# The state-space output map multiplied into the cell's input weights on chip, and later states made between the cell's steps

## The reference, cut to what matters

```python
    def _L2_cond_ref(x, conv_w, conv_b, Wp, bp, Ws, bs, A_log, dt_log, Wo, bo):
        conv = conv_b + sum((x_pad[:, k:k + L, :] * conv_w[k, 0] for k in range(K)))
        proj = conv @ Wp + bp
        B_t = jax.nn.softplus(proj[..., :N])
        C_t = jnp.tanh(proj[..., N:])
        u = x @ Ws + bs
        def step(state, inputs):
            state = decay * state + dt * b_t * u_t
            return (state, c_t * state)
        y = jnp.swapaxes(ys, 0, 1)
        return y @ Wo + bo

    def _L2_ffn_ref(x, wf, uf, bf, wi, ui, bi, wc, uc, bc, wo, uo, bo, in_c):
        def step(c, xt):
            ft = jax.nn.sigmoid(xt @ wf.T + c @ uf.T + bf)
            it = jax.nn.sigmoid(xt @ wi.T + c @ ui.T + bi)
            gt = jnp.tanh(xt @ wc.T + c @ uc.T + bc)
            c = ft * c + it * gt
            return (c, None)
        c_final, _ = lax.scan(step, c0, x)
        h = jnp.tanh(jnp.einsum('tbi,oi->tbo', x, wo) + c_final @ uo.T + bo)
```

## Time and profile before

| what | before |
|---|---|
| median of 3 runs | 3221.84 us (3221.58 to 3226.26) |
| time of the profiled execution | 3220.31 us |
| its span | 3218.6 us |
| TensorE busy | 88% of the span |
| DVE, ACT, POOL busy | 43%, 27%, 13% |
| mean granted TensorE clock | 0.764 of full speed |
| share of the chain that ended last: PE | 76% |

### The profile page before, as it was taken

One profiled execution on the slowest core, in us unless ns is written; L12 is line 12 of the kernel. 1 busy time (PEld: TensorE's weight loads), 2 busy tenths in 40 slices (PEclk: granted clock), 3 DMA queues, 4 the chain that ended last, 5 costly groups with the idle time before them and its releaser, 6 DMA issues.

```text
span 3218.6 us, 73352 instructions
## 1 busy us (share of the span) xinstructions
PE 2819.7 (88%) x28032; PEld 2120.7 (66%) x28032; DVE 1385.8 (43%) x6805; ACT 867.4 (27%) x2721; POOL 404.5 (13%) x477
## 2 busy tenths in 40 slices
PE   7888888888888888439999998999979997999788
PEld 5777777777777777128888887556843342586467
DVE  5555555555555555201111111664435565412532
ACT  1222222222222222222322222113533222322332
POOL 1000000000000000341111111333420000001333
PEclk6555555555555555659999998999989999899999
DMA  9990000000000000146666666223453210000023
GB/s 312 379 354 4 2 2 2 2 2 2 2 2 2 2 2 2 47 134 203 195 184 206 190 189 190 90 75 96 138 168 126 104 54 0 0 0 0 28 82 102
DMA packets 218204, 295.94 MB, mean 92 GB/s; under 512 B 57688, under 2 KB 160704, under 8 KB 216704
## 3 DMA queue, kind: packets, MB, share of 16 engines
q1 hardware_dynamic: 200640, 243.80, 23.1%
q0 software_dynamic: 17344, 48.78, 4.2%
HBM read 167.59 MB, written 124.94 MB: 91 GB/s over the span
## 4 chain that ended last, share of the span: by engine, by line
PE 76%; DVE 8%; ACT 6%; issue 4%; POOL 3%; DMA 1%; SPq 0%; DVEq 0%; POOLq 0%; ACTq 0%
PE bank L1548 20%; PE bank L1656 8%; PE bank L1668 8%; PE bank L1532 8%; PE bank L1932 5%; PE bank L1740 4%; ACT gate_r L663 3%; DVE rhpart L992 3%; PE bank L1838 3%; PE bank L1882 3%; PE bank L1791 2%; PE bank L1802 2%; POOL tile_rows L607 2%; PE bank L2033 2%; PE bank L2045 2%
## 5 line engine op out<-in xcount | busy, mean ns | idle before, releaser
L1548 PE MATMUL bank<-h_high,WB 128*128 128x8 f16 x9216 | 422.3, 169 | 87.2 <-DVE h_high L1008 67.3
L1548 PEld LDWEIGHTS bank<-h_high,WB 128*128 128x128 f16 x9216 | 335.6, 105 | 204.3 <-DVE h_high L1008 165.7
L1548 PE MATMUL bank<-rhpart,WB 128*128 128x8 f16 x6144 | 288.2, 171 | 84.6 <-DVE rhpart L992 84.6
L1548 PEld LDWEIGHTS bank<-rhpart,WB 128*128 128x128 f16 x6144 | 242.8, 106 | 130.0 <-DVE rhpart L992 127.9
L1656 PE MATMUL bank<-WA,WB 128*128 128x256 f32 x1248 | 310.3, 382 | 7.3 <-DMA WA<-in_L_ffn_b 7.3
L1668 PE MATMUL bank<-WB,hid 128*128 128x256 f32 x1248 | 313.9, 379 | 0.0
L1532 PE MATMUL bank<-XT,WB 128*128 128x128 f32 x792 | 304.5, 482 | 0.0
L1548 PE MATMUL bank<-h_low,WB 128*128 128x8 f16 x4608 | 299.5, 171 | 0.0
L1656 PEld LDWEIGHTS bank<-WA,WB 128*128 128x128 f32 x1248 | 238.7, 191 | 40.5 <-issue 7.7
L725 ACT ACTIVATE hid<-bank,b_up 128x256 f32<-128x256 f32 x312 | 148.0, 474 | 395.4 <-PE bank L1656 395.4
L1668 PEld LDWEIGHTS bank<-WB,hid 128*128 128x128 f32 x1248 | 234.4, 190 | 30.4
(11 more groups left out here) (352 smaller groups left out, 4091.6 us busy)
## 6 DMA issues: line engine op xcount, KB each, us to landing
WB<-in_L_ffn_w SPq DMA_DIRECT2D x78, 1024.0 KB, 7.8
tile_rows<-WA SPq DMA_DIRECT2D x32, 2176.0 KB, 19.5
WA<-tile_rows SPq DMA_DIRECT2D x78, 272.0 KB, 2.9
GB<-gates SPq DMA_DIRECT2D x8, 2048.0 KB
WA<-expert_rows SPq DMA_DIRECT2D x16, 512.0 KB, 5.7
WB<-expert_rows SPq DMA_DIRECT2D x16, 512.0 KB, 7.9
WA<-in_L_ffn_b SPq DMA_DIRECT2D x40, 128.0 KB, 8.2
GB<-in_x SPq DMA_DIRECT2D x8, 512.0 KB, 7.4
```

The source lines that it names most:

```text
L1548: last = nc.tensor.matmul(bank[:, m * width + s * B:m * width + (s + 1) * B], wpart[:, g, w, k, m * P:(m + 1) * P], part[a][:, k * B:(k + ...
```

## The change

The product of `Wo` (with its bias `bo` as a 65th row) and each of wf, wi, wc and wo is made once on chip, four 65x256 matrices `wz`. The cell's input products and the output product then read the states directly: a 65-row operand `ssm_y1`, 64 rows of state and a row of ones written by POOL. The `Wo` product over all tokens is gone. The turning of the cell weights and the start of `c2` now stand ahead of the projections. The projections B and C are one product of 128 output rows, banks are used four batches deep, and ACT takes both B and C. The last tile's taps stand between the batches, three ahead. Four states are made before the cell's loop, the other four inside it, after the DVE work of half steps 0 to 3; DVE's loop is written out for that.

```diff
-        ssm_c, ssm_b, ssm_u = GB[0:NS, 0:4096], GB[0:NS, 4096:8192], HT[0:NS, 0]
+        ssm_u, ssm_c = HT[0:NS, 0], HT[0:NS, 1]
+        ssm_y1 = WA[0:NS + 1, 4096:8192]
+        ssm_b = ssm_y1[0:NS]
+        woT = hidf[:, 1024:1024 + KD * (NS + 1)].rearrange("p (k n) -> p k n", k=KD)
+        wz = GB[0:NS + 1, 7168:8192].rearrange("p (g m) -> p g m", g=4)
...
+            pool.wait_ge(uT_psum, 9)
+            nc.gpsimd.memset(ssm_y1[NS:NS + 1], 1.0).then_inc(prefer_ready, 1)
...
-            act.sem_inc(ssm_taken[1], 1)
+            for g in range(4):
+                act.wait_ge(wz_psum, g + 1)
+                nc.scalar.copy(wz[:, g], banks[g][0:NS + 1, 0:D]).then_inc(wz_ready, 1)
             for h in range(2):
                 for j in range(h * HB, (h + 1) * HB):
-                    act.wait_ge(p2_psum, j * 3 + 2)
-                    nc.scalar.activation(ssm_c[:, j * TILE:(j + 1) * TILE], banks[1][0:NS], ACT.Tanh, bias=small2[:, 3:4]
-                                         ).then_inc(ssm_taken[1], 1)
+                    act.wait_ge(p2_psum, j * 2 + 1)
+                    nc.scalar.activation(ssm_b[:, c], bank[0:NS], ACT.Identity, bias=small_all[0:NS, 2:3]).then_inc(ssm_taken[0], 1)
+                    nc.scalar.activation(ssm_c[:, c], bank[NS:2 * NS], ACT.Tanh, bias=small_all[NS:2 * NS, 2:3]).then_inc(ssm_taken[0], 1)
...
-            for j in range(B):
-                for m in range(KD):
-                    n = j * KD + m
-                    act.wait_ge(y_psum, n + 1)
-                    nc.scalar.activation(HT[:, m, j * TILE:(j + 1) * TILE], banks[n % 4][:], ACT.Identity,
-                                         bias=bo2[:, m:m + 1]).then_inc(z_ready2, 1)
...
+            dve.wait_ge(uT_psum, 1)
+            V.tensor_copy(woT[:, :, 0:NS], banks[0][:, 0:KD * NS].rearrange("p (k n) -> p k n", k=KD))
+            V.tensor_copy(woT[:, :, NS:NS + 1], bo2[:].rearrange("p (k n) -> p k n", n=1)).then_inc(uT_ready, 1)
...
+            for tap in range(3):
+                conv_tap(NTILE - 1, tap)
+            for j in range(B):
+                if j + 3 < B:
+                    conv_tap(NTILE - 1, j + 3)
+                c = slice(j * TILE, (j + 1) * TILE)
+                dve.wait_ge(p2_psum, j * 2 + 2)
+                V.tensor_scalar(ssm_u[:, c], banks[j % 4 * 2 + 1][0:NS], small2[:, 3:4], dt, ALU.add, ALU.mult).then_inc(ssm_taken[1], 1)
+                if j > HB:
+                    state_space(j - HB - 1)
+            state_space(HB - 1)
...
                     V.scalar_tensor_tensor(c2h, a, 0.5, b, ALU.mult, ALU.add).then_inc(cell_ready, 1)
+                    if n < HB:
+                        state_space(HB + n)
...
+            pe.wait_ge(uT_ready, 5)
+            for g in range(4):
+                for k in range(KD):
+                    last = nc.tensor.matmul(banks[g][0:NS + 1, 0:D], woT[:, k], uT[:, g, k], start=k == 0, stop=k == KD - 1)
+                last.then_inc(wz_psum, 1)
+            pe.wait_ge(wz_ready, 4)
+            pe.wait_ge(uT_ready, 9)
+            for j in range(B):
+                for k in range(KD):
+                    pe.wait_ge(conv_step[k], B * (j + 1))
+                if j >= 4:
+                    pe.wait_ge(ssm_taken[0], (j - 3) * 2)
+                    pe.wait_ge(ssm_taken[1], j - 3)
+                for w, bank, src in ((wp2, banks[j % 4 * 2], HT), (ws2, banks[j % 4 * 2 + 1], XT)):
+                    o = bank[:] if w is wp2 else bank[0:NS]
...
             with pe.Fori(0, B) as j:
+                pe.wait_ge(ssm_y, j + 1)
...
+                                if not part:
+                                    nc.tensor.matmul(o, wz[:, g, half_of(m)], ssm_y1[:, bass.ds(j * TILE + h * 256, 256)],
+                                                     start=m == 0, stop=False, skip_group_check=True)
...
-                        for k in range(KD):
-                            last = nc.tensor.matmul(banks[i * 2 + m][:], uT[:, 3, k, half_of(m)], HT[:, k, cols(j2 * 2 + i)],
-                                                    start=k == 0, stop=k == KD - 1)
-                        last.then_inc(o2_psum, 1)
+                        nc.tensor.matmul(banks[i * 2 + m][:], wz[:, 3, half_of(m)], ssm_y1[:, cols(j2 * 2 + i)],
+                                         start=True, stop=True).then_inc(o2_psum, 1)
```

More of the change, by code:

```diff
@@ L297, in build_program @@
         up_copied, down_copied = sem("up_copied"), sem("down_copied")
-        p2_psum, ssm_taken = sem("p2_psum"), [sem(f"ssm_taken{i}") for i in range(3)]
-        softplus_log, ssm_y, y_psum, z_ready2 = sem("softplus_log"), sem("ssm_y"), sem("y_psum"), sem("z_ready2")
+        p2_psum, ssm_taken = sem("p2_psum"), [sem(f"ssm_taken{i}") for i in range(2)]
+        softplus_log, ssm_y, wz_psum, wz_ready = sem("softplus_log"), sem("ssm_y"), sem("wz_psum"), sem("wz_ready")
         uT_psum, uT_ready = sem("uT_psum"), sem("uT_ready")
@@ L1351, in _ @@
             dt = small2[:, 8:9]
-            dve.sem_inc(ssm_taken[0], 1)
-            dve.sem_inc(ssm_taken[2], 1)
             def state_space(j):
@@ L1887, in _ @@
             for k in range(KD):
-                pe.wait_ge(conv_step[k], B * NTILE)
-            for j in range(B):
-                for x, w in enumerate((wp2[:, :, 0:NS], wp2[:, :, NS:2 * NS], ws2)):
-                    pe.wait_ge(ssm_taken[x], j + 1)
-                    for k in range(KD):
-                        last = nc.tensor.matmul(banks[x][0:NS], w[:, k], (HT if x < 2 else XT)[:, k, j * TILE:(j + 1) * TILE],
-                                                start=k == 0, stop=k == KD - 1)
-                    last.then_inc(p2_psum, 1)
-            for x in range(3):
-                pe.wait_ge(ssm_taken[x], B + 1)
-            for j in range(B):
-                pe.wait_ge(ssm_y, j + 1)
-                for m in range(KD):
-                    n = j * KD + m
-                    if n >= 4:
-                        pe.wait_ge(z_ready2, n - 3)
-                    nc.tensor.matmul(banks[n % 4][:], wo2[:, half_of(m)], ssm_b[:, j * TILE:(j + 1) * TILE], start=True, stop=True
-                                     ).then_inc(y_psum, 1)
+                last = nc.tensor.transpose(banks[0][:, k * NS:(k + 1) * NS], wo2[:, half_of(k)], ident[0:NS, 0:NS])
+            last.then_inc(uT_psum, 1)
             pe.wait_ge(uraw_loaded, 8 * 16)
@@ L1915, in _ @@
                 last.then_inc(uT_psum, 1)
-            pe.wait_ge(uT_ready, 8)
-            pe.wait_ge(z_ready2, 2 * B)
+            pe.wait_ge(uT_ready, 5)
[5 more added lines that the diff above has]
+            pe.wait_ge(uT_ready, 9)
+            for j in range(B):
+                for k in range(KD):
[5 more added lines that the diff above has]
+                    o = bank[:] if w is wp2 else bank[0:NS]
+                    for k in range(KD):
+                        last = nc.tensor.matmul(o, w[:, k], src[:, k, j * TILE:(j + 1) * TILE], start=k == 0, stop=k == KD - 1)
+                    last.then_inc(p2_psum, 1)
+            pe.wait_ge(ssm_taken[0], 2 * B)
+            pe.wait_ge(ssm_taken[1], B)
+            pe.wait_ge(prefer_ready, 2 * E + 8)
             with pe.Fori(0, B) as j:
+                pe.wait_ge(ssm_y, j + 1)
                 for h in range(2):
@@ L1929, in _ @@
                             for m in range(KD):
-                                for k in range(KD):
-                                    src = c2[:, k, h * 256:(h + 1) * 256] if part else HT[:, k, bass.ds(j * TILE + h * 256, 256)]
-                                    last = nc.tensor.matmul(banks[h * 3 + g][:, m * 256:(m + 1) * 256],
-                                                            uT[:, g + 4 * part, k, half_of(m)], src,
-                                                            start=not part and m == 0 and k == 0, stop=part == 1, skip_group_check=True)
+                                o = banks[h * 3 + g][:, m * 256:(m + 1) * 256]
+                                if not part:
+                                    nc.tensor.matmul(o, wz[:, g, half_of(m)], ssm_y1[:, bass.ds(j * TILE + h * 256, 256)],
+                                                     start=m == 0, stop=False, skip_group_check=True)
+                                else:
+                                    for k in range(KD):
+                                        last = nc.tensor.matmul(o, uT[:, g + 4, k, half_of(m)], c2[:, k, h * 256:(h + 1) * 256],
+                                                                start=False, stop=True, skip_group_check=True)
                             if part:
```

53 lines of the change are left out of this document (17 added, 36 removed).

## The result

| what | before | after |
|---|---|---|
| median of the runs | 3223.28 us (3221.58 to 3226.26, 4 runs) | 3125.65 us (3125.09 to 3128.5, 4 runs) |
| ratio, with its 95% interval | | 0.9698 [0.9681, 0.9715] |
| profiled execution, span | 3220.31, 3218.6 us | 3125.09, 3123.3 us |
| mean granted TensorE clock | 0.764 | 0.759 |

The account below looks back on a forecast made before the run. Preparation was taken as a chain of engines waiting in turn, the cell loop as all PE. Savings of 50.6 (preparation), 41.6 (loop) and 5 us (output product) sum to 97.2: 3221.84 - 97.2 = 3124.6 us, range 3115 to 3138.

Parts of the forecast that it names:

- rival B: Preparation: the clock falls while the weights are turned ahead of `wz`, 4.5 us more, 3129 us; chance 0.08.
- 32 x 0.867 = 27.7: Preparation: 32 projection matmuls instead of 48, at 0.867 us each, take 27.7 us.
- and only then does it release the first part 0: Preparation: ACT releases the cell loop only when its second softplus ends at 2730.2, so the loop starts at 2730.3.
- the 8 us of cover: Preparation: DVE makes batch 7's eighth tap 8 us before PE needs it; POOL's memset could use up to 3.7.
- PE stays the bound: Cell loop: ACT and DVE need 6.4 us with a state ahead, against 10.4 available, so PE still sets the time.
- rivals C: Cell loop: the clock falls and rises with the 65-row third, 96 matmuls at half clock, 41.5 us, 3166; chance 0.06.
- D: Cell loop: the clock falls and stays at half, 124.4 us more, 3247, slower than before; chance 0.03.
- E: Cell loop: ACT or DVE take over as the bound, the 41.6 us saving doesn't come, 3166; chance 0.02.
- the 1.6 us for the start: Start of the cell loop: PE starts at half clock after standing idle and loses 1.6 us, as before the change.
- ends 0 and 9.5: Output product: bounds of the gain, 0 us at half clock and 9.5 at full clock; 5 us was taken.
- so I let the clock fall after 5 us: Output product: full clock for 5 us, then half; the next block starts after 29.8 us instead of 34.67.
- rival A: Output product: the 65-row product keeps the full clock, gaining 9.5 us instead of 5, 3120.1 us; chance 0.20.

Follow-up runs that it names:

- u_wide: Changed kernel with the u product of the projections given 128 output columns instead of 64, the upper 64 output rows never read; 3123.54 us, ratio 0.9695.
- double_in: Changed kernel with every input product of the cell loop issued twice, 96 more matmuls of 65 rows; 3169.6 us, ratio 0.9831.
- rows128: Changed kernel with the cell's input products and the output product reading 128 rows instead of 65, the extra rows leftover data; 3122.33 us, ratio 0.9685.
- release_early: Changed kernel with ACT releasing the cell's first input products before its second softplus instead of after it; 3121.44 us, ratio 0.9689.
- wo_back: Changed kernel with all eight states first, then the `Wo` product and ACT's 16 copies put back, result unused; 3152.56 us, ratio 0.9779.
- rows64: Changed kernel with those products reading 64 rows instead of 65 (no bias row) and PE's loops over the batches written out; 3133.42 us, ratio 0.9719.
- scales_early: Changed kernel with DVE preparing the next block's scales ahead of the output product instead of after it; 3120.64 us, ratio 0.9689.
- all_three: Changed kernel with the diffs of u_wide, release_early and scales_early together; 3119.41 us, ratio 0.9679.

## Why the prediction was right, point by point

**Preparation: 46.8 predicted, 45.1 measured; two errors that offset each other.** The turning and `wz` came as predicted: `wz` is 3.47 us for 3.45, projections start 11.2 us after the last add for 11.7. The clock was 1.00 while PE did nothing but transposes, so rival B fell. The Trainium skill, "TensorE: Matmul & The Clock Gate", Part 4, says that the full clock doesn't engage for them; here the measurement decides:

```profile
2686.60:2692.20 5.60, 4.88 (x34) 3.56 (x35) 4.60 (x9) 0.00 (x0) 0.00 (x0) 1.00 0.01 3
```

The first error is the price of the projections, "32 x 0.867 = 27.7": they took from 2696.31 to 2726.6, 30.3 us, which is 2.6 more. The price was right for two matmuls of one shape; between 128 and 64 output columns a change costs 0.17 us, and u_wide took it away. The second is "and only then does it release the first part 0". ACT's last pass of the second softplus runs after PE has been released:

```profile
2730.25 4.76 PE L1934 MATMUL bank<-WA,GB 65*128 x12 [3.67 <-ACTq L890]
...
2731.35 1.91 ACT L888 ACTIVATE WB<-WB 64x2048 f32<-64x2048 f32 x1
```

The increment of `gate2_ready` is an instruction of ACT's sequencer, with no data of its own. It took effect at 2730.25, 3.0 us before the last Ln ended (2733.26). I had put it behind that end.

DVE and POOL held nothing up. POOL's memset of the ones (2692.46, 3.50 us for 1 by 4096 elements, against 3.72 for 128 by 4352 in the earlier trace rows) did hold DVE: L1354, 64 by 2 elements, took 2.95 us and ended with it, as the prediction feared, and the 8 us of cover paid for it.

**Cell loop: 126.0 predicted, 128.0 measured.** The term for the steady part is right, 7.77 us per half step, and so is "PE stays the bound" (double_in); rivals C, D and E fell, by a clock of 1.00 over 119 busy us:

```profile
2739.00:2858.20 119.20, 119.20 (x553) 104.49 (x551) 42.47 (x61) 40.02 (x94) 0.00 (x0) 1.00 0.00 0
```

Mis-sized is the 1.6 us for the start, taken over from before. The first half step took 11.41 us (4.76 + 6.65), so 3.6 was lost:

```profile
2731.10:2737.80 6.70, 6.70 (x18) 5.26 (x17) 3.25 (x5) 3.43 (x3) 0.00 (x0) 0.50 0.01 2
```

Before, the half clock held for 3.2 us, and the loop began with 128-row operands. Now its first six matmuls have 65 rows. rows128 shows that their depth matters: the clock was back after 4.7 us, and 1.7 of the 2.0 us came back. release_early agrees, since there the 65-row matmuls ran mostly before the fall and 1.9 us was lost. It is not depth alone: u_wide lost 5.0 us with the same six, its clock having fallen before the loop began. What sets the moment of the fall these runs don't show. Nor did PE start low, as the prediction had it: it started at 1.00 and fell 0.8 us later.

**Output product: 5 predicted of ends 0 and 9.5, 7.5 measured.** The step that failed is "so I let the clock fall after 5 us". It never fell, which is rival A:

```profile
2867.30:2880.00 12.70, 12.64 (x29) 5.53 (x30) 7.61 (x11) 6.79 (x11) 9.96 (x9) 1.00 0.00 0
```

L1905 was the wrong nearest row, though as shallow. Why it lost its clock and the output product didn't is open. Before, PE had waited 1.10 us ahead of L1905, and the clock fell 2.3 us into work without a break, ahead of the next wait of 1.51:

```profile
2744.20:2746.40 2.20, 2.20 (x6) 0.99 (x7) 2.13 (x3) 2.17 (x2) 0.00 (x0) 1.00 0.00 0
2746.60:2749.00 2.40, 2.39 (x3) 0.33 (x1) 0.56 (x1) 2.39 (x2) 0.00 (x0) 0.50 0.00 0
```

Here the clock had fallen in the 2.98 us ahead of `uo`, `uo`'s full-depth matmuls brought it back, and 0.96 us of pause follow, hardly less than the 1.10:

```profile
2861.20:2863.00 1.80, 1.76 (x2) 0.84 (x3) 0.00 (x0) 0.00 (x0) 0.00 (x0) 0.50 0.00 0
...
2866.40:2867.30 0.90, 0.00 (x0) 0.00 (x0) 0.00 (x0) 0.68 (x1) 0.00 (x0) 1.00 0.00 0
```

wo_back kept 1.00 through 3.67 us of 64-row work behind a pause of 1.41 us, and had 0.50 behind one of 2.46. So the rows alone don't decide, since rows64 kept the clock too; that a pause does was not tried in the output product, and the lengths above don't sort by themselves. What holds in all of them is that shallow work at 0.50 didn't bring the clock back (L1905, wo_back), and shallow work without a break behind a full clock and a pause under 1 us kept it.

But A's own 9.5 was too much by 2. The last sum ended 18.3 us behind PE's start, for 19.0 in A; PE was done after 14.6, and POOL's adds were the bound. I had taken the tail of 6.2 us behind that sum as given, and it grew to 8.9, since DVE's L1409 ran beside POOL's queue of adds. Before, the same instruction was L1410 and took 0.51 us. PE had twice the matmuls per piece, all at a clock of 1.00, and gave POOL one piece in 1.72 us, so POOL stood idle 0.45 us behind each add and had no queue:

```profile
2985.25 1.26 POOL L625 TENSOR_TENSOR XT<-XT,GB 128x512 f32 x1 [0.45 <-ACT GB L902]
...
2986.04 0.51 DVE L1410 TENSOR_SCALAR ys<-condT 128x16 f32<-128x16 f32 x1
```

Even there DVE ended with POOL's add (2986.55, POOL 2986.51), so it was held for the rest of that one. scales_early got 3.4 us back by moving it. The Trainium skill, "SBUF — State Buffer", "SBUF: two separate sides", says that DVE in its fast modes, or with two inputs in SBUF, and POOL share a port pair, which one of them holds for a whole instruction. The trace agrees that they exclude each other, but shows more: DVE was held over some three of POOL's adds of 1.23 us, until its queue ran dry.

**Outside the sum: +4.2 us.** The stretch ahead of the last add varies by 6 us between executions of one code. The rest has the same code as well and grew by 2.55. Followed down the chain, 1.1 of that lies 60 to 94 us into it, where the chain runs through POOL, DMA and ACT; PE's clock was lower there too, but PE is not on the chain. 1.2 more lies just behind, where PE is the chain and stayed longer at half clock. Before, and then after:

```profile
3086.13 1.10 PE bank L2020 x4
...
3088.00 4.43 PE bank L2033 x12
```

```profile
2989.66 1.10 PE bank L2023 x4
...
2991.53 5.49 PE bank L2036 x12
```

All thirteen profiles of the changed kernel and its versions have 227.3 to 230.5 there, the one profile of the kernel before 226.3. In all_three the same twelve records took 4.23 us and the rest 227.3, so part of this varies from one execution to the next. What made the 1.1 us on POOL and DMA longer I didn't try to settle.

So 3124.6 against 3125.65 is closer than its terms, and that is luck: -1.7 in the preparation, +2.0 in the loop, -2.5 in the output product, +4.2 outside. Several of the prediction's own signs did not show: PE idle for 7 us ahead of the loop (3.7), the softplus ending ahead of it (3.0 us behind), projections at 3.47 us (3.78), the clock at 1.00 from the loop's fourth microsecond (from its eighth), and the clock falling in the output product (never). The range of 3115 to 3138 covered each of the four errors alone and their sum.

## What to carry to other kernels

Fold a linear map into the weights behind it when its result is read by nothing else: the gain is the product itself plus what waited in line with it, and on an engine that is the bound each matmul taken away gives its full time. Then look at the restart: where PE pauses ahead of a stretch, shallow products at its head cost up to 2 us here, so deeper ones first may be worth a try (I did not reorder any), and read the clock window by window, since 1.4 of 2.1 us won ahead of a pause were lost behind it. And when PE gets faster, look for DVE's smallest instructions beside POOL's longest queue.

## What the runs showed of the hardware

- A change of the stationary tile's shape at full clock costs 0.17 us between 128 and 64 columns (u_wide) and 0.19 between 128 and 64 rows (rows64); 65 rows against 128 cost nothing (7.77 us a half step in both). The Trainium skill, "TensorEngine Tiling (Array Packing)", Key Properties, has it that a mode switch requires a drain; a price at each change fits that, though the trace shows the time and not the drain.
- Operands of 64 and 65 rows kept the full clock in unbroken work (12.3 and 12.7 us at 1.00), but once the clock was at half they hardly brought it back: 0.51 over 20.5 busy us in wo_back. At the loop's start it was back after 4.7 us with none of them at the head, 7.6 and 9.7 with six (the changed kernel, u_wide), 14 with twelve.
- A DVE instruction of 128 by 16 elements that reads SBUF takes 4.20 us beside a queue of POOL adds, 0.51 beside the end of a single one, and 0.17 without; one that reads PSUM at the same time (L1407) takes 0.69 and isn't held.
- A semaphore increment of ACT's sequencer took effect 3.0 us before the activation ahead of it in the code ended.
- POOL's memset costs by columns: 1 by 4096 elements 3.50 us, 128 by 4352 3.72.
